# A three-layer cross network on one core: first tiles by two queues, single-tile signals, squares first, and GpSimd's gathers and the squares of step 2 in another place

## What is computed

```
x0 = xk = e                                  # (2048, 32, 16)
for W in (W0, W1, W2):                       # (32, 32|64, 64)
    xk = relu(einsum('bmd,bhd,mhk->bkd', x0, xk, W))
    outs.append(sum(xk, axis=2))
z = concatenate(outs, axis=1)                # (2048, 192)
h = concatenate([z, dense_ctx], axis=1)
h = maximum(h @ W_top1 + b_top1, 0);  h = maximum(h @ W_top2 + b_top2, 0);  y = h @ W_top3
```

## Time and profile before

| | |
|---|---|
| median of three runs | 1191.82 us |
| the profiled execution's own time | 1192.97 us |
| its span in the trace | 1191.2 us |
| busy, share of the span | TensorE 94%, VectorE 94%, GpSimd 77%, ScalarE 62% |
| mean granted TensorE clock | 0.991 of full |
| DMA | 167.25 MB, 140 GB/s over the span |

### The profile page before, as it was taken

One profiled execution on the slowest core, in us unless ns is written; L12 is line 12 of the kernel. 1 busy time (PEld: TensorE's weight loads), 2 busy tenths in 40 slices (PEclk: granted clock), 3 DMA queues, 4 the chain that ended last, 5 costly groups with the idle time before them and its releaser, 6 DMA issues.

```text
span 1191.2 us, 14658 instructions
## 1 busy us (share of the span) xinstructions
PE 1121.3 (94%) x5312; PEld 393.6 (33%) x5312; DVE 1118.8 (94%) x521; ACT 733.9 (62%) x1361; POOL 918.8 (77%) x640
## 2 busy tenths in 40 slices
PE   0488899999999999999999999999999999999997
PEld 0122223333333333333333333333333333333333
DVE  0487999999999999999999999999999999999995
ACT  0343666676667667665766766576676657657653
POOL 6688888888888888888888888888888888885400
PEclk9888999999999999999999999999999999999999
DMA  5887787667678766677876666788666778876300
GB/s 110 190 176 146 158 171 155 138 132 144 140 157 171 157 141 141 132 144 150 172 163 136 143 134 145 144 171 168 139 140 134 143 145 169 166 144 144 61 1 1
DMA packets 76216, 167.25 MB, mean 140 GB/s; under 512 B 21776, under 2 KB 39072, under 8 KB 76144
## 3 DMA queue, kind: packets, MB, share of 16 engines
q1 hardware_dynamic: 59216, 161.95, 64.8%
q0 software_dynamic: 16384, 4.23, 3.6%
q10 hardware_dynamic: 544, 0.14, 0.1%
HBM read 157.86 MB, written 8.40 MB: 140 GB/s over the span
## 4 chain that ended last, share of the span: by engine, by line
PE 86%; POOL 3%; DVE 3%; DMA 3%; issue 3%; ACT 1%; SPq 1%; DVEq 0%
PE acc L600 80%; POOL x_rows L254 3%; DVE p_dve L516 3%; PE acc L672 3%; PE acc L658 1%; PE acc L660 1%; DMA q_tile<-x_of_steps 1%; ACT xb L317 1%; DMA x_rows<-in_table,ids_s 1%; PE acc L680 1%; DMA spread<-x_of_steps 1%; SPq L192 1%; DMA x_of_steps<-x_rows 0%; SPq L219 0%; DVE z L543 0%
## 5 line engine op out<-in xcount | busy, mean ns | idle before, releaser
L600 PE MATMUL acc<-p_dve,w_s 128*64 128x512 f32 x3840 | 863.2, 598 | 22.5 <-DVE p_dve L516 21.8
L254 POOL DMA_INDIRECT x_rows<-in_table,ids_s x512 | 493.7, 964 | 146.1 <-issue 131.2
L516 DVE TENSOR_TENSOR p_dve<-spread,xb 128x3072 f32<-128x3072 f32 (+2 forms) x224 | 572.2, 2682 | 2.9 <-issue 2.9
L516 DVE TENSOR_TENSOR p_dve<-spread,xa 128x2048 f32<-128x2048 f32 (+1 forms) x192 | 501.5, 2730 | 16.6 <-issue 9.1
L600 PEld LDWEIGHTS acc<-p_dve,w_s 128*64 128x64 f32 x3840 | 267.9, 137 | 571.5 <-issue 467.2
L317 ACT ACTIVATE xb<-acc 32x512 f32<-32x512 f32 x512 | 288.8, 564 | 71.6 <-DVE p_dve L516 65.5
L266 POOL TENSOR_TENSOR p_l<-spread,q_tile 128x2048 f32<-128x2048 f32 x60 | 272.7, 4573 | 11.0 <-DMA q_tile<-x_of_steps 10.4
L308 ACT ACTIVATE xa<-acc 64x512 f32<-64x512 f32 x256 | 145.9, 570 | 189.6 <-PE acc L600 155.0
L277 POOL TENSOR_TENSOR p_pool<-spread,x_s 128x1024 f32<-128x1024 f32 x64 | 152.2, 2378 | 94.7 <-PE acc L600 45.9
L600 PE MATMUL acc<-p_l,w_s 128*64 128x512 f32 (+1 forms) x640 | 152.5, 612 | 41.6 <-DVE p_l L556 41.6
L326 ACT ACTIVATE x_s<-acc 64x512 f32<-64x512 f32 x256 | 151.5, 592 | 8.3 <-ACT y_row L449 4.8
(11 more groups left out here) (18 smaller groups left out, 151.1 us busy)
## 6 DMA issues: line engine op xcount, KB each, us to landing
spread<-x_of_steps SPq DMA_DIRECT2D x248, 512.0 KB, 17.4
q_tile<-x_of_steps SPq DMA_DIRECT2D x128, 128.0 KB, 11.4
x_rows<-in_table,ids_s POOLq DMA_INDIRECT x512
x_of_steps<-x_rows SPq DMA_DIRECT2D x64, 128.0 KB
spread<-x_of_steps SPq DMA_DIRECT2D x16, 256.0 KB, 5.4
w_s<-in_w SPq DMA_DIRECT2D x2, 512.0 KB, 5.7
wt<-in_w_top SPq DMA_DIRECT2D x1, 512.0 KB, 6.5
z_all<-in_dense_t ACTq DMA_DIRECT2D x16, 8.0 KB, 8.2
```

Source lines behind the costliest of these rows:

```text
L254: nc.gpsimd.indirect_dma_start(out=x_rows[:, s % 2, i * DIM:(i + 1) * DIM], out_offset=None, in_=table, in_offset=bass.IndirectOffsetOnAxi ...
L516: nc.vector.tensor_tensor(p_dve[:, to:to + n, :], spread[:, s % 3, tile:tile + n, :], over(x[:], n), ALU.mult).then_inc(dve_made, n)
L600: last = nc.tensor.matmul(acc[b * K:(b + 1) * K, :], w, prod[:, b * BLK:(b + 1) * BLK], start=start, stop=stop)
```

## The change

- Step 0's q_tile and tiles come by two queues: SyncE issues quarters 0 and 1, ScalarE quarters 2 and 3, ahead of its first squares. Later steps stay with SyncE.
- In steps 0 and 1 each of tiles 0 to 3 is a transfer and a signal of its own, and VectorE makes the products tile by tile.
- layer0 starts with the squares and ends with the fourth product, in every step.
- layer0(1) stands after chunk 10 of L1(0) instead of 13, and its products after the same chunk on VectorE.
- GpSimd waits for x1_a(0), then gathers all of step 2, and only then makes product(0, 1) and product(1, 1); 8 gathers follow (up to number 56) where 12 did (up to 60), and the 4 left out come after first_layer_products(2). TensorE takes GpSimd's chunk of step 0 after chunk 14 in both layers (before: 9 and 11).
- ScalarE makes squares(2) after x2_b(0) instead of ahead of it.

The diff, cut:

```diff
+SP_QUADS, ACT_QUADS = (0, 1), (2, 3)
+POOL_AFTER_OF_0 = 14
-L0_OF_1_AFTER = 13
+L0_OF_1_AFTER = 10
+GATHERED_IN_TURN_0 = 56
@@ SyncE
             def load_tiles(s, first_tile, n, signal):
-                for q in range(Q):
+                for q in SP_QUADS if s == 0 else range(Q):
...
                 if s < 2:
-                    load_tiles(s, 0, NA // 2, half_a_loaded[s])
-                    load_tiles(s, NA // 2, NA - NA // 2, a_loaded[s])
+                    for i in range(NA - 1):
+                        load_tiles(s, i, 1, tile_loaded[s][i])
+                    load_tiles(s, NA - 1, 1, a_loaded[s])
...
             def load_q(s):
-                for q in range(Q):
+                for q in SP_QUADS if s == 0 else range(Q):
@@ GpSimd
             gathers(0, 2 * XI)
+            pool.wait_ge(x1a_ready, 1)
+            gathers(2 * XI, 3 * XI)
             product(0, 1)
-            gathers(2 * XI, 3 * XI)
             product(1, 1)
-            gathers(3 * XI, gathers_before(1))
+            gathers(3 * XI, GATHERED_IN_TURN_0)
             for s in range(1, STEPS):
                 n = gathers_before(s)
                 if s + 1 < STEPS:
                     first_layer_products(s + 1)
-                gathers(n, n + THEN)
+                gathers(n if s > 1 else GATHERED_IN_TURN_0, n + THEN)
@@ ScalarE
+            act.wait_ge(x_stored, 32)
+            for q in ACT_QUADS:
+                act.dma_start(q_tile[q * FIELDS:(q + 1) * FIELDS, :],
+                              scratch[0, 0:FIELDS, :]).then_inc(q_loaded, 16)
+            for i in range(NA - 1):
+                load_tiles(i, 1, tile_loaded[0][i])
+            load_tiles(NA - 1, 1, a_loaded[0])
+            load_tiles(NA, NT - NA, b_loaded[0])
             act.wait_ge(w_loaded, LOADED)
             squares(0)
...
-                if s + 1 < STEPS:
+                if s != 1 and s + 1 < STEPS:
                     squares(s + 1)
...
                 if s >= 1:
                     x2_b(s - 1)
+                if s == 1:
+                    squares(2)
@@ VectorE
-                for c in 0, 2:
-                    if c == 2:
+                for c in range(CP):
+                    if c < CP - 1:
+                        dve.wait_ge(tile_loaded[s][c], 16 * Q)
+                    else:
                         dve.wait_ge(a_loaded[s], 16 * Q)
-                    nc.vector.tensor_tensor(p_l0[:, c:c + 2, :], spread[:, s % 3, c:c + 2, :],
-                                            over(q_tile[:], 2), ALU.mult).then_inc(l0_made, 2)
+                    nc.vector.tensor_tensor(p_l0[:, c, :], spread[:, s, c, :], q_tile[:],
+                                            ALU.mult).then_inc(l0_made, 1)
@@ TensorE
-                for c in range(C0):
+                for c in CP, *range(CP):
...
-                if c == POOL_AFTER_L1:
+                if c == (POOL_AFTER_L1 if s > 0 else POOL_AFTER_OF_0):
...
-                if c == POOL_AFTER_L2:
+                if c == (POOL_AFTER_L2 if s > 0 else POOL_AFTER_OF_0):
```

More of the change, by code:

```diff
@@ L137, in build_kernel @@
         q_loaded = sem("q_loaded")
-        half_a_loaded = [sem(f"half_a{s}_loaded") for s in range(2)]
+        tile_loaded = [[sem(f"tile{i}_of_step{s}_loaded") for i in range(NA - 1)] for s in range(2)]
         a_loaded = [sem(f"a_loaded{u}") for u in range(3)]
@@ L451, in mlp3, with load_tiles @@
                 act.dma_start(y[:, t * P:(t + 1) * P], y_row[:]).then_inc(y_stored, 16)
-            load_dense(0)
+            def load_tiles(first_tile, n, signal):
+                for q in ACT_QUADS:
+                    o = Q * first_tile + q + 1
+                    first = scratch[0, o:o + 1, :]
+                    src = bass.AP(first.tensor, first.offset, [[COLS, FIELDS], [Q * COLS, n], [1, COLS]])
+                    act.dma_start(spread[q * FIELDS:(q + 1) * FIELDS, 0, first_tile:first_tile + n, :],
+                                  src).then_inc(signal, 16)
+            load_dense(0)
+            act.wait_ge(x_stored, 32)
+            for q in ACT_QUADS:
+                act.dma_start(q_tile[q * FIELDS:(q + 1) * FIELDS, :],
[4 more added lines that the diff above has]
+            load_tiles(NA, NT - NA, b_loaded[0])
             act.wait_ge(w_loaded, LOADED)
@@ L549, in first_layer_products @@
                 dve.wait_ge(q_loaded, 16 * Q * (s + 1))
-                dve.wait_ge(half_a_loaded[s], 16 * Q)
                 if s > 0:
                     dve.wait_ge(l0_used, C0 * s)
-                for c in 0, 2:
-                    if c == 2:
+                for c in range(CP):
+                    if c < CP - 1:
+                        dve.wait_ge(tile_loaded[s][c], 16 * Q)
+                    else:
                         dve.wait_ge(a_loaded[s], 16 * Q)
-                    nc.vector.tensor_tensor(p_l0[:, c:c + 2, :], spread[:, s % 3, c:c + 2, :],
-                                            over(q_tile[:], 2), ALU.mult).then_inc(l0_made, 2)
+                    nc.vector.tensor_tensor(p_l0[:, c, :], spread[:, s, c, :], q_tile[:],
+                                            ALU.mult).then_inc(l0_made, 1)
             dve.wait_ge(ids_loaded, 32)
@@ L607, in layer0 @@
                     pe.wait_ge(mlp_done, mlp_evictions)
-                for c in range(C0):
+                for c in CP, *range(CP):
                     rows = P if c < CP else FIELDS
-                    if c == 0 and s > 0:
+                    if c == CP and s > 0:
                         pe.wait_ge(x1b_ready, s)
@@ L616, in layer0 @@
                         pe.wait_ge(squares_made, s + 1)
-                    contract(acc0, w0_s[0:rows, c, :], p_l0[0:rows, c, :], c == 0, c == C0 - 1
+                    contract(acc0, w0_s[0:rows, c, :], p_l0[0:rows, c, :], c == CP, c == CP - 1
                              ).then_inc(l0_used, 1)
```

## The result

Measured: 1187.13 us median (1186.51 to 1190.19, 6 executions) against 1192.15 us of the kernel before (1191.42 to 1193.62), ratio 0.9962 (95% interval 0.9949 to 0.9974). Faster, by 5.0 us, where the forecast said 10.7 (1181.5). The profiled execution took 1190.19 us.

What follows compares the result with a forecast made beforehand. TensorE and VectorE are full from 300 to 400 us, so gains lie in the first 150 us. Terms 5.4 + 2.9 + 2.4 = 10.7 us gave 1182.3 from the profiled 1192.97, stated as 1181.5; range 1178.8 to 1187.5.

Steps and rivals of the forecast that it cites:

- Term 2: VectorE's wait ahead of xb of L2(0): moving squares(2) behind x2_b(0) removes 2.89 us.
- term 3: VectorE's wait ahead of L1(2): 3.5 of 5.88 us stays, 2.4 us gained, with TensorE staying at 2.4 GHz.
- Term 1: Start of VectorE's L1(1): faster step 0 loads land step 1's last gather and tiles sooner, 5.4 us earlier.
- x1_a(1) is no limit: Step 1, layer 0: one TensorE chunk (1.64) and 2.31 after 66.7 make 70.7, ahead of L1(1) at 72.3.
- T1: The time at which VectorE starts L1(1): 77.68 us in the kernel before, forecast at 72.3.
- before tiles 0 to 2 have all landed: VectorE reaches step 1's layer 0 products at 58 to 60, so step 0's 4.4 to 6 us are hidden, counting 0.
- first rival: Step 0's loads: two queues gain nothing in rate; sum 6.2, 1186; chance 0.17.
- that rival's sign, the store of step 1 at 52.6: SyncE's store of step 1 still at 52.6 instead of near 48 would show no gain in rate.
- two places at zero room: x2_b(1): xb of L2(1) ready at 135.7, wanted at 135.4; p_l(3): made at 139.6, TensorE waits 1.8 us.
- second rival: GpSimd or q_tile of step 3 takes back part, p_l(2) coming after 101: 1183 to 1186; chance 0.18.
- the forecast's own remark: SyncE's queue is full with step 1's tiles until about 74.4, so q_tile of step 2 lands at 92.
- The rate: Step 0's loads by two queues: taken as 289 GB/s, where one queue showed 222.

Runs made afterwards that it cites:

- 7: Changed kernel with squares(2) put back ahead of x2_b(0): 1184.98 us, ratio 0.995 to the kernel before.
- series 5: Repeat on one chip, prompt signals: changed kernel unchanged 1185.04 us (0.994); changed kernel without GpSimd's wait for x1_a(0) 1183.43 us (0.9928).
- 8: Changed kernel with GpSimd's order as in the kernel before: 1183.86 us, ratio 0.993; repeated in series 4: 1187.14 us, 0.9947.
- 9: Changed kernel without GpSimd's wait for x1_a(0): 1183.41 us, ratio 0.9929; repeated in series 5: 1183.43 us, 0.9928.
- series 4: Repeat with late signals: changed kernel unchanged 1187.74 us (0.9958), changed kernel with GpSimd's order as before 1187.14 us (0.9947), and experiment 12.
- experiment 12: Kernel before with only step 0's loads by two queues (tiles in pairs) and squares(2) behind x2_b(0): 1189.25 us, ratio 0.996.
- Experiment 4: Changed kernel with SyncE alone issuing step 0's transfers, one tile each: 1193.87 us, ratio 1.0007.
- 6: Changed kernel with tiles 4 to 7 of step 1 loaded only after x1_a(1): 1196.16 us, one execution.
- 10: Changed kernel with one signal of TensorE for a whole layer 0 instead of one per chunk: 1186.47 us, ratio 0.995.

## Why the prediction was wrong

- *Terms 2 and 3* came to the tenth in the first trace: x2_b(0) at 93.76 (forecast 93.9), waits 0 and 3.51. But part of term 3 is chance: the unchanged kernel before waited 3.88 and 5.04 in two more traces where the first had 5.88. Term 2 needs the squares' move: with them ahead, 1.83 us of wait came back even with GpSimd's early gathers (7).
- *Term 1* is the step that failed: "x1_a(1) is no limit: one chunk of TensorE ... and 2.31 after 66.7 make 70.7." It took the hand-over from matmul to ScalarE as 0.05 us, as the only trace showed it, and had 1.6 us of room. In the changed kernel's first trace the hand-over was 3.35 us, and the end of layer 0 came 3.8 us behind the last product instead of 1.64; T1 came at 76.66, 4.4 us after the forecast. The second goes back to the first gap: x1_a(0) at 48.55 put VectorE to step 1's products at 62.47, where the forecast had 58 to 60, "before tiles 0 to 2 have all landed". There it waited for none of the four tiles, so the 4.1 us of the first gap were no longer hidden behind them, and TensorE was behind with L1(0). Where signals are prompt (series 5) the step is right: one chunk, 1.13 us, after the last product, x1_a(1) at once, and T1 at 70.38, 1.9 us ahead of what I reckoned.
- *The size of the miss.* L1(2) was 6.4 us earlier and not 10.7, VectorE kept these 6.4 to 1160 us, and the median gained 5.0. This looks like the first rival (sum 6.2, 1186) and lies within the stated range, but by luck: that rival's sign, the store of step 1 at 52.6, is absent (it went out at 47.49), and the range was drawn for other causes.
- *"So the sum stands with two places at zero room"* failed where term 1 held. The first place cost VectorE 1.49 us (x2_b(1)), and TensorE waited 1.73 at p_l(3), for which I had 1.8. TensorE's longest wait there, 3.85 us, was not in my list at all: I counted the four moved gathers only as four fewer ahead of p_l(2), and not as four more ahead of product(0,2). 2.9 us of 12.0 were given back by 190 us. The time (1185.04) falls in my second rival's 1183 to 1186, but its cause is not the one that I named: p_l(2) was made at 101.45, as reckoned (101), and a part of the time is the tail below.
- *GpSimd's wait and early gathers* bring nothing: undone whole (8) or without the wait (9), the kernel is not slower but 0.6 us (series 4) and 1.6 us (series 5) faster, within the intervals. With prompt signals q_tile of step 2 landed between 92.2 and 92.6 us in all of these. Its last gather was issued anywhere from 66.0 to 71.2 (after 7.51 us it landed at 74.90 in series 5), and the store waited for it until 73.9 to 75.0, about when step 1's last tiles landed. SyncE had issued those tiles by 62. That the tiles hold up q_tile of step 2 was the forecast's own remark, and its price should have been followed.
- *The rate* was right: 267 to 313 GB/s from 34 to 44 us with two queues in the first trace, against 198 to 222 of the kernel before (in series 4 the changed kernel had 215 to 253, and experiment 12, with pairs of tiles, 279 to 312). Experiment 4 doesn't test it, since its slow issues set its rate. With the second queue the transfers of quarters 0 and 1 and those of 2 and 3 are also issued at the same time and no longer in turn, and no run separates this from the second issuer. By the Trainium skill, "DMA: Bandwidth & Descriptors", section "Rules for kernel authors", spreading over issuing engines brings no bandwidth; here the two queues, with the quarters split between them, brought it, and the measurement decides.
- *The tail* (the last 30 us): in series 5 the lead at VectorE's sums near 1160 us is 8.9 us (1157.11 against 1166.02), but from there to the end it took 26.6 us and not 25.2, with matmuls at half clock. That leaves 7.5, the difference of the two profiled executions (1192.97 and 1185.47). I had no term for it.

Left open is what makes TensorE's signals late in some series. At x1_a(1) it was not tiles in flight (6, one execution), and not the chip's number alone: two series with the same one differ. The number of signals is untested (10 ran among prompt ones and so tells nothing), and so are squares first (see 12) and the recording itself: every time here is that of a recorded execution, so no run shows whether the signals are late without it. The best version by the medians, within the intervals, is the changed kernel with GpSimd's order as before or without its wait, 1183.4 to 1183.9 with prompt signals.
